# One stage for the choice of the 32 largest values of a row and for the dense sum over its neighbours

## The reference

```python
def _maxk(x, k):
    _, idx = jax.lax.top_k(x, k)
    rows = jnp.arange(x.shape[0])[:, None]
    mask = jnp.zeros_like(x).at[rows, idx].set(1.0)
    return x * mask
h_self = feat @ W_self
h_neigh = feat @ W_neigh
h_sparse = _maxk(h_neigh, 32)
summed = jax.ops.segment_sum(h_sparse[src], dst, num_segments=n)
deg = jax.ops.segment_sum(jnp.ones((src.shape[0],)), dst, num_segments=n)
return h_self + summed / jnp.maximum(deg, 1.0)[:, None]
```

## Time and profile before

| | us |
|---|---|
| median of 3 runs | 7333.49 |
| lowest and highest | 7317.44, 7339.35 |
| the profiled execution | 7353.0 |
| its span | 7351.3 |
| PE busy in the span | 5270.3 (72%) |
| DVE busy | 4191.8 (57%) |
| ACT busy | 2271.7 (31%) |
| POOL busy | 1431.6 (19%) |
| granted clock of PE, mean | 0.862 |

### The profile page before, as it was taken

How to read it: one execution, slowest core, us unless ns; L and a number is a source line. 1 busy time by engine, 2 the same in 40 slices (tenths; PEclk the granted TensorE clock), 3 DMA queues, 4 the chain that set the end, 5 groups by cost and what they waited for, 6 DMA issues and landing times. The chain is left out here.

```text
span 7351.3 us, 77634 instructions
## 1 busy us (share of the span) xinstructions
PE 5270.3 (72%) x21589; PEld 3572.6 (49%) x21589; DVE 4191.8 (57%) x6678; ACT 2271.7 (31%) x4039; POOL 1431.6 (19%) x1466
## 2 busy tenths in 40 slices
PE   0222778879788689989878747849955777767976
PEld 0000344444444366668767536738843333336754
DVE  6200399964999732233387361021128999997857
ACT  0000211112111033322254212212226777765611
POOL 0677066630666300001000000020020000000000
PEclk9755889889899889999989878969977888888978
DMA  1111433445334400004331002245644444433200
GB/s 27 27 36 36 199 97 100 111 105 234 107 101 112 84 15 17 9 20 122 107 128 63 13 5 54 56 140 180 185 121 132 155 156 154 150 106 124 83 13 17
DMA packets 379940, 679.42 MB, mean 92 GB/s; under 512 B 94754, under 2 KB 306908, under 8 KB 372157
## 3 DMA queue, kind: packets, MB, share of 16 engines
q1 hardware_dynamic: 304364, 519.11, 21.8%
q0 software_dynamic: 75344, 157.40, 8.3%
HBM read 503.61 MB, written 172.62 MB: 92 GB/s over the span
## 5 line engine op out<-in xcount | busy, mean ns | idle before, releaser
L605 POOL DMA_INDIRECT sum_rows_in<-rel_table,rel_row x880 | 849.7, 966 | 451.3 <-issue 236.9
L629 DVE TENSOR_SCALAR sum_hot_cell<-x_nodes 128x1500 bf16<-128x1500 f16 (+1 forms) x880 | 892.9, 1015 | 2.8 <-issue 2.8
L683 PE MATMUL ps<-sum_hot_cell,sum_hot_src 128*128 128x500 bf16 x2640 | 779.6, 400 | 157.7 <-issue 85.5
L1592 PE MATMUL ps<-att_ring,acc 125*65 125x500 f32 x1000 | 607.2, 693 | 305.1 <-DVE att_ring L1414 304.9
L552 PE MATMUL ps<-rel_diag,rel_xt 128*128 128x512 f32 x800 | 433.4, 690 | 408.0 <-ACT rel_stage L511 178.4
L688 PE MATMUL ps<-sum_rows_in,sum_hot 128*128 128x256 f32 x1760 | 597.7, 419 | 59.4 <-issue 52.2
L1600 PE MATMUL ps<-acc,att_ring 125*125 125x257 f32 x2500 | 569.7, 391 | 72.4 <-DVE att_ring L1414 44.9
L785 PE MATMUL ps<-aux,sum_wide 125*125 125x256 f32 x2500 | 580.6, 388 | 49.8 <-ACT sum_wide L734 49.8
L1530 ACT ACTIVATE att_ring<-att_ring,att_src 125x625 f32<-125x625 f32 x750 | 545.4, 804 | 126.2 <-DVE att_ring L1395 126.2
L1395 DVE TENSOR_TENSOR att_ring<-att_ring,att_rows 125x3125 f32<-125x3125 f32 (+1 forms) x162 | 512.6, 3170 | 101.6 <-ACT att_ring L1489 100.5
L1489 ACT ACTIVATE att_ring<-att_rows,att_src 125x625 f32<-125x625 f32 x750 | 547.9, 804 | 34.7 <-PE ps L1600 33.5
(11 more groups left out here) (430 smaller groups left out, 7349.1 us busy)
## 6 DMA issues: line engine op xcount, KB each, us to landing
att_cell<-cells SPq DMA_DIRECT2D x150, 781.2 KB, 4.7
att_masks<-masks SPq DMA_DIRECT2D x150, 762.9 KB
rel_table<-rel_stage SPq DMA_DIRECT2D x50, 2048.0 KB, 6.3
ffn_w<-in_L_ffn_W SPq DMA_DIRECT2D x64, 1024.0 KB, 7.4
sum_cell<-cells SPq DMA_DIRECT2D x250, 156.2 KB, 2.3
masks<-sum_stage POOLq DMA_DIRECT2D x25, 762.9 KB, 11.9
sum_rows_in<-rel_table,rel_row POOLq DMA_INDIRECT x880
cells<-x_nodes SPq DMA_DIRECT2D x5, 2031.2 KB
```

The source lines that it names most:

```text
L605: pool.indirect_dma_start(rows_in[:, b, u, :], None, table, bass.IndirectOffsetOnAxis(rows[:, k:k + 1], 0)).then_inc(gathered[b], 16)
L629: dve.tensor_scalar(hot_cell[:, b, u, :], K.columns[:, :, 0:CW], K.cell[:, k], None, ALU.is_equal).then_inc(s_hot, 1)
L683: pe.matmul(K.ps[:, bass.ds(side * 4 + j, 1), 0:BW].rearrange("p a n -> p (a n)"), hot_src[:, b, u, :], hot_cell[:, b, u, j * BW:(j + 1) * ...
L1592: pe.matmul(K.ps[0:W, side, 0:BAND], node_rows[s][0:NPT, h, :], ring[0:NPT, b % RB, v, 0:BAND], start=s == 0, stop=s == NT - 1).then_inc(s ...
```

## The change

The node pass "sage" and the sum "sum4" are replaced by one stage, `best_and_sum`, tag "sage". What each engine computes is the same; these things differ:

- ACT copies all 512 columns of a product to SBUF, to y, which has ten buffers; DVE chooses from y and POOL adds from y. The products have two PSUM banks (6 and 7), the transposes one (5), xt four buffers.
- PE works through k = 0 to 34: turn(k + 1), multiply(k), and from k = 10 on the cell (0, k - 10), for which it waits until the rows of that source tile are chosen. The 100 cells of the other four target groups follow.
- ACT casts cells between its copies, four ahead of PE's use. SP loads them from the start of the stage.
- Every product of a cell signals, and each of the five banks is copied out as soon as its own last product is there; PE waits for each bank alone.
- The cells are written out; there is no loop over groups any more. DVE's order of work is as before.

```diff
--- before.py
+++ after.py
@@ -1010,6 +1010,207 @@
                 mm.then_inc(s_mm, 1)
                 if t + LAG < NT:
                     turn(t + LAG)
+
+def best_and_sum(K, tag, neigh_name, own_name):
+
+    nc = K.nc
+    NG5 = NT // UN
+    NB = NG5 * NT
+    XB, TB2, YB, CB, AHEAD = 2 * UN, 4, 2 * UN, UN, UN - 1
+    LAG = YB
+    with Phase(nc, tag) as ph:
+        loaded, s_stats, s_aggr, s_var, s_rstd, s_inv = (ph.sem(n) for n in ("loaded", "stats", "aggr", "var", "rstd", "inv"))
...
+        w_sb = ph.sb("w", [P, DC, 2 * D])
+        stats, mv = ph.sb("stats", [P, NT, 6]), ph.sb("mv", [P, NT, 2])
+        xin, xt = ph.sb("xin", [P, XB, D]), ph.sb("xt", [P, TB2, DC, P])
+        y, work, best = ph.sb("y", [P, YB, 2 * D]), ph.sb("work", [P, UN, D]), ph.sb("best", [P, UN, 8])
+        cell, wide = ph.sb("cell", [P, CB, GW], U16), ph.sb("wide", [P, CB, GW])
+        block = ph.block()
+        ps_t = K.ps[:, 5, 0:D]
+
+        def ps_y(t):
+
+            return K.ps[:, 6 + t % 2, :]
+
+        @block.sync
+        def _(sp):
+            for n, name in enumerate((neigh_name, own_name)):
+                sp.dma_start(w_sb[:, :, n * D:(n + 1) * D], K.inp[name].rearrange("(c p) n -> p c n", p=P)).then_inc(loaded, 16)
+            for c in range(NB):
+                if c >= CB:
+                    sp.wait_ge(s_wide, c - CB + 1)
+                sp.dma_start(cell[:, c % CB, :], K.cells[c // NT, c % NT, :, :]).then_inc(cell_in[c % CB], 16)
+
+        @block.vector
+        def _(dve):
...
+            def write(i):
+
+                var = mv[:, i * UN:(i + 1) * UN, 1]
+                dve.wait_ge(s_rstd, i + 1)
+                dve.reciprocal(var, var).then_inc(s_inv, 1)
+                dve.wait_ge(s_inv, i + 1)
+                if i >= 2:
+                    dve.wait_ge(s_tr, (i - 1) * UN)
+                for t in range(i * UN, (i + 1) * UN):
+                    dve.tensor_scalar(xin[:, t % XB, :], K.x[:, t, :], mv[:, t, 0:1], mv[:, t, 1:2],
+                                      ALU.subtract, ALU.mult).then_inc(s_pre, 1)
+
+            def choose(i):
+
+                tiles = range(i * UN, (i + 1) * UN)
+                h = {t: work[:, t % UN, :] for t in tiles}
+                top = {t: best[:, t % UN, :] for t in tiles}
+                row = {t: y[:, t % YB, 0:D] for t in tiles}
+                for t in tiles:
+                    dve.wait_ge(s_kept, t + 1)
+                    dve.max(top[t], row[t]).then_inc(s_best, 1)
+                dve.wait_ge(s_best, (i + 1) * UN)
+                link.all([dve.match_replace(h[t], top[t], row[t], -BIG) for t in tiles])
+                for _ in range(MAXK // 8 - 1):
+                    link.all([dve.max(top[t], h[t]) for t in tiles])
+                    link.all([dve.match_replace(h[t], top[t], h[t], -BIG) for t in tiles])
+                for t in tiles:
+                    dve.scalar_tensor_tensor(out=K.aux[:, t, :], in0=h[t], scalar=-BIG, in1=row[t],
+                                             op0=ALU.is_equal, op1=ALU.mult).then_inc(s_post, 1)
+
+            measure(0)
+            measure(1)
+            for i in range(NG5):
+                write(i)
+                if i + 2 < NG5:
+                    measure(i + 2)
+                if i > 0:
+                    choose(i - 1)
+            choose(NG5 - 1)
+
...
+        @block.scalar
+        def _(act):
+
...
+            def turned(t):
+
+                act.wait_ge(s_tr, t + 1)
+                if t >= TB2:
+                    act.wait_ge(s_y, t - TB2 + 1)
+                act.copy(xt[:, t % TB2, :, :], ps_t.rearrange("p (c f) -> p c f", c=DC)).then_inc(s_xt, 1)
+
+            def keep(t):
+
+                act.wait_ge(s_y, t + 1)
+                if t >= YB:
+                    act.wait_ge(s_post, t - YB + 1)
+                    act.wait_ge(s_own, t - YB + 1)
+                act.copy(y[:, t % YB, :], ps_y(t)).then_inc(s_kept, 1)
+
+            def widen(c):
+
+                act.wait_ge(cell_in[c % CB], (c // CB + 1) * 16)
+                if c >= CB:
+                    act.wait_ge(s_mm, (c - CB + 1) * UN)
+                act.copy(wide[:, c % CB, :], cell[:, c % CB, :]).then_inc(s_wide, 1)
+
+            def evict(g):
+
+                for u in range(UN):
+                    act.wait_ge(s_mm, ((g + 1) * NT - 1) * UN + u + 1)
+                    act.copy(K.acc[0:NPT, g * UN + u, 0:D], K.ps[0:NPT, u, 0:D]).then_inc(s_out, 1)
+
+            root(0)
+            root(1)
+            turned(0)
+            for k in range(NT + LAG):
+                if k % UN == UN - 1 and 1 <= k // UN < NG5 - 1:
+                    root(k // UN + 1)
+                if k + 1 < NT:
+                    turned(k + 1)
+                if k < NT:
+                    keep(k)
+                c = k - LAG + AHEAD
+                if c >= 0:
+                    widen(c)
+            evict(0)
+            for c in range(NT, NB):
+                if c + AHEAD < NB:
+                    widen(c + AHEAD)
+                if c % NT == NT - 1:
+                    evict(c // NT)
+
+        @block.tensor
+        def _(pe):
+
+            def turn(t):
+
+                pe.wait_ge(s_pre, t + 1)
+                if t > 0:
+                    pe.wait_ge(s_xt, t)
+                for c in range(DC):
+                    mm = pe.transpose(ps_t[:, c * P:(c + 1) * P], xin[:, t % XB, c * P:(c + 1) * P], K.ident[:, :])
+                mm.then_inc(s_tr, 1)
+
+            def multiply(t):
+
+                pe.wait_ge(s_xt, t + 1)
+                if t >= 2:
+                    pe.wait_ge(s_kept, t - 1)
+                for c in range(DC):
+                    mm = pe.matmul(ps_y(t), xt[:, t % TB2, c, :], w_sb[:, c, :], start=c == 0, stop=c == DC - 1)
+                mm.then_inc(s_y, 1)
+
+            def gather(c):
+
+                g, s = c // NT, c % NT
+                pe.wait_ge(s_wide, c + 1)
+                if g == 0:
+                    pe.wait_ge(s_post, s + 1)
+                for u in range(UN):
+                    if s == 0 and g > 0:
+                        pe.wait_ge(s_out, (g - 1) * UN + u + 1)
+                    pe.matmul(K.ps[0:NPT, u, 0:D], wide[0:NPT, c % CB, u * NPT:(u + 1) * NPT], K.aux[0:NPT, s, :],
+                              start=s == 0, stop=s == NT - 1).then_inc(s_mm, 1)
+
+            turn(0)
+            pe.wait_ge(loaded, 32)
+            for k in range(NT + LAG):
+                if k + 1 < NT:
+                    turn(k + 1)
+                if k < NT:
+                    multiply(k)
+                if k >= LAG:
+                    gather(k - LAG)
+            for c in range(NT, NB):
+                gather(c)
 
 
 def normed(K):
@@ -2447,33 +2648,7 @@
         add_normed(K, "res1b", "L1_ffn_gamma", "L1_ffn_beta")
 
 
-        def max_k(dve, link, i, ps_y, s_mm, s_post, tools):
-            tiles = range(i * UN, (i + 1) * UN)
-            h = {t: tools.work[:, t % UN, :] for t in tiles}
-            best = {t: tools.best[:, t % UN, :] for t in tiles}
...
-            for t in tiles:
-                dve.scalar_tensor_tensor(out=K.aux[:, t, :], in0=h[t], scalar=-BIG, in1=ps_y(t)[:, 0:D],
-                                         op0=ALU.is_equal, op1=ALU.mult).then_inc(s_post, 1)
-
-        def own_rows(act, t, ps, tools):
-            if t >= UN:
-                act.wait_ge(tools.s_ppost, t - UN + 1)
-            return act.copy(tools.own[:, t % UN, :], ps[:, D:2 * D])
-
-        def add_own(pool, t, tools):
-            return pool.tensor_tensor(K.x[:, t, :], K.x[:, t, :], tools.own[:, t % UN, :], ALU.add)
-
-        node_pass(K, "sage", ["L2_gnn_W_neigh", "L2_gnn_W_self"], [], normed(K), norm=lambda t: K.x[:, t, :],
-                  post=max_k, act_post=own_rows, pool_post=add_own)
-        dense_sum(K, "sum4", K.aux)
+        best_and_sum(K, "sage", "L2_gnn_W_neigh", "L2_gnn_W_self")
         add_mean(K, "res2")
 
 
```

More of the change, by code:

```diff
@@ L1012, in _, with measure, root @@
                     turn(t + LAG)
+def best_and_sum(K, tag, neigh_name, own_name):
[6 more added lines that the diff above has]
+        loaded, s_stats, s_aggr, s_var, s_rstd, s_inv = (ph.sem(n) for n in ("loaded", "stats", "aggr", "var", "rstd", "inv"))
+        s_pre, s_tr, s_xt, s_y, s_kept, s_best = (ph.sem(n) for n in ("pre", "tr", "xt", "y", "kept", "best"))
+        s_post, s_own, s_wide, s_mm, s_out, step = (ph.sem(n) for n in ("post", "own", "wide", "mm", "out", "step"))
+        cell_in = [ph.sem(f"cell_in{b}") for b in range(CB)]
+        w_sb = ph.sb("w", [P, DC, 2 * D])
[17 more added lines that the diff above has]
+        def _(dve):
+            link = Chain(dve, step)
+            def measure(i):
+                tiles = range(i * UN, (i + 1) * UN)
+                for t in tiles:
+                    dve.bn_stats(stats[:, t, :], K.x[:, t, :]).then_inc(s_stats, 1)
+                for t in tiles:
+                    dve.wait_ge(s_stats, t + 1)
```

(30 more changed lines are left out.)

## The result

| | before | changed |
|---|---|---|
| median, us | 7333.4 | 7226.7 |
| lowest and highest | 7317.4, 7339.4 | 7220.0, 7233.5 |
| span of the profiled execution | 7351.3 | 7224.5 |

The ratio of the medians is 0.9858 (95% interval 0.9840 to 0.9876): 107 us faster, where 97 were forecast. The range held it.

A forecast was written before the change was run, and what follows sets the result against it. DVE bound the choosing, PE the sum. DVE's stage 25.1, way to first remaining product 7.9, hidden cells 43.2, pauses 10.8, starts 9.2, evictions 0.9: 97 us off 7333.5 gives 7236 us, range 7216 to 7262.

The forecast's parts named there:

- Hidden cells: Twenty cells of the sum, run beside DVE's choosing: 43.2 us saved.
- Pauses between target groups: Four pauses of 2.71 us in the old sum go, since banks are evicted singly: 10.8 us saved.
- Start at half clock: Old sum had five starts at half clock, 2.3 us each; one stays: 9.2 us saved.
- (a): Choosing: copying y with 512 columns, not 256, takes ACT 586 ns against 377; 0.2 us later per row.
- (b): Last operation of DVE's choice reads both operands from SBUF: 0 to 0.33 us per group, 0.33 taken.
- (c): Sum: signals on all 625 products, not every fifth, and written-out code instead of a loop; price nothing.
- (d): Choosing: transposes with one PSUM bank, not three, products two, not five; 0.25 us in the first tiles.
- (e): Joined stage: POOL's add and the cell loads (DMA, 2.2 us to landing) stay beside the rest.
- The walk: Timed steps through the joined stage from 4320.5: choice 0 ends 4355.9, choice 4 4438.0, last eviction 4665.9.
- 1 and 4 (signals): Rivals on the sum's products: 1, each signal delays the next, saving 86, chance 0.07; 4, overlap lost, 107 slower, chance 0.03.
- 2 (no overlap): Rival, joined stage: queue order holds every cell behind the last choice; saving 52 us, 7281; chance 0.05.
- 3 (no upper clock): Rival, joined stage: upper clock not granted while DVE sets the pace; saving 29 us, 7304; chance 0.05.

The follow-up runs named there:

- the second measurement: Changed kernel again, no edit: stretch 346.5 us, ratio 0.9877 against the kernel before.
- apart: Changed kernel, but every cell waits for the end of the last choice: stretch 389.7 us, ratio 0.9920 against before.
- evict_together: Changed kernel, but ACT copies the five banks after the group's last product and PE waits for all five copies: stretch 355.0 us, ratio 0.9882 against before.
- y5_root: Changed kernel with five buffers for y instead of ten and ACT taking each root five tiles earlier: stretch 376.8 us.
- few_signals: Changed kernel with one signal per cell, except the last cell of a target group: stretch 346.6 us, ratio 0.9860 against before.
- lag12_root: Changed kernel with cells twelve tiles behind instead of ten and roots five tiles earlier: stretch 348.1 us, ratio 0.9866 against before.
- warm: Changed kernel plus unread products in PE's idle time, ahead of the first transposes and tile 10's: stretch 345.7 us, ratio 0.9866 against before.
- early_write: Changed kernel with DVE writing and measuring ahead of the choice instead of behind it, roots earlier: stretch 339.7 us, ratio 0.9843 against before.
- y5: Changed kernel with five buffers for y instead of ten, cells still ten tiles behind: stretch 381.1 us, ratio 0.9915 against before.

## Why the prediction was right

**The whole.** The sum was 97, the stretch gave 97.4. The medians gave 107 and, in the second measurement, 90; the allowance of 11 us for their scatter was about right.

**Terms.** Hidden cells, 43.2 us: apart, 43.3. Pauses between target groups, 10.8: evict_together gives back 7.6 with the casts still ahead; the other part was the cast, which the new order makes ahead. Start at half clock, 9.2: in the changed kernel one of five is left, at 1.8 us where the sum had 2.3, and evict_together shows that pauses of 1.66 us cost none. DVE's stage ends 25.1 us earlier: 142.7 to 116.4, 26.3. The buffer behind it is worth 30 us by y5_root.

**Prices.** (a) The copy of 512 columns took 586 ns, as its row said, but it does not come later to DVE. In the old kernel ACT copied the next tile's xt ahead of the own half; now the copy to y stands first:

```profile
4338.75 0.38 ACT L2469 COPY sage_own<-ps 128x256 f32<-128x256 f32 x1
4317.19 0.59 ACT L1135 COPY sage_y<-ps 128x512 f32<-128x512 f32 x1 [1.08 <-PE ps L1188]
4317.81 0.43 DVE L1088 MAX8 sage_best<-sage_y 128x8 f32<-128x256 f32 x1 [1.51 <-ACT sage_y L1135]
```

For tile 4 the old copy ended at 4339.13, 0.9 us behind its product, the new one at 4317.78, 0.6 behind. (b) wrong: five of the last operation with both operands in SBUF take 1.77 us against 1.75, not 2.07. I had taken L2195 as the nearest row because its operands lie where the new ones do. What slows L2195 is something else; it also reads a scalar from memory per row, which was not tried apart. (c) right, and shown by few_signals. (d) With one bank for the transposes the first tile's pair of products started 0.34 us later, but took 3.31 us where it had taken 3.60: PE was 0.05 us late, not 0.25. (e) hidden, as said, but for one meeting with POOL (last section).

The walk was 1.0 us late at choice 0. Of that 0.7 is the fifth row, which came at 18.5 us where (a) and (d) had put it at 19.1, and 0.3 is (b). From there on forecast and trace run side by side, 1.1 to 1.3 us apart.

**What I had missed.** A wait of 1.2 us for a root, and 1 us more between the last eviction and the mean: 4645.73 - 4643.54 = 2.2, against 4764.22 - 4762.99 = 1.2. Of this 0.6 is the barrier's clearing of semaphores by SP, one after another at 0.057 us each: 23 in the joined stage, 12 in sum4. Both made up for what the walk had put in too much. Between choices 2 and 3, for example, the root's 1.2 us were balanced by 0.3 of (b) and by the wait for tile 19, which was 0.7 shorter than forecast. So the agreement to 0.4 us in the end is partly luck, and so is some of that at each choice; the structure (who waits for whom, and where) is as forecast.

**Rivals.** 1 and 4 (signals) fell with few_signals. 2 (no overlap) was built as apart, and saves 54 us, where its price was 52. 3 (no upper clock) fell with the profile: 0.97 over the layer. Two sums of the prediction are wrong as they stand. In rival 4, 204 us less 97 is 107 slower, which is 7440 and not 7340. In rival 3, 3.9 + 15 x 8.2 from 4356.4 is 4483 and not 4479. The bounds of the range, too, are 3 and 5 us wider than the terms given for them (7219 to 7257); the result, 7226.7, lies inside either.

## What to carry to other kernels

Two stages, each bound by another engine, are worth joining, but here more than half of the gain was not the overlap: it was a second set of buffers in front of the slower engine, a barrier, and pauses at the changes of group. Once joined, keep one account of the idle time of the engine that is now the bound, over the whole joined stretch. Work taken from the place where it fills a gap cost 1.7 us (lag12_root), and 1.7 us saved ahead of a wait came to 0.7 (warm); letting the other engine hand over its next rows before it starts its long job brought 5.0 (early_write).

Measure such a change on its own stretch of the trace. It repeated to 0.1 us, where the medians of the whole program moved by 10.

## What the runs showed of the hardware that I had not expected

- Behind a pause of 1.66 us of PE the upper clock stayed (54.19 us for the next 250 records), as behind 1.28 in the earlier trace rows. Behind 2.43 or 2.44 us it went both ways. In the changed kernel it fell: the granted clock was 0.50 from 4415 to 4418, and the first 1050 records took 228.55 us, 1.8 more than 105 x 2.158 and the last record's 0.17. The same wait cost the clock in six of the other kernels too. In early_write it stayed at 1.00 and the 1050 records took 226.86 us. In both PE had been without a pause for over 50 us, at 1.00. So the length of the pause alone does not decide it; what else does stays open.
- Behind the pause of 9.42 us the second tile was slow too (2.40 us for its pair), though PE had been busy since 4334.33; the granted clock was 0.50 from 4334 to 4339.
- One of the 25 last operations of DVE lasted 947 ns, where the median is 418, in the changed kernel (the row of 2.29 us). An addition of POOL runs beside it:

```profile
4354.04 0.87 POOL L1112 TENSOR_TENSOR x_nodes<-x_nodes,sage_y 128x256 f32<-128x256 f32 x1 [3.37 <-ACT sage_y L1135]
```

So it is wherever it happens. Over the twelve profiles of the table, 16 of the 300 last operations took 504 to 952 ns, and each had an addition of POOL beside it, 15 of them for 0.66 us; the other 284 took at most 427. It costs 0.5 us a time: once here, in four groups of five with y5, and not at all with warm or lag12_root, where the additions fall beside other operations. MAX8 and MATCH_REPLACE8 took no longer beside an addition (at most 430 and 414 ns) than without. The old kernel's last operations, with one operand in PSUM, had no addition beside them, so whether the place of the operand matters is not shown. This is one of the signs of being wrong that the prediction named, DVE's choice slower beside other engines' traffic; it came true at a size of 0.5 us.
